# Projection slots of the next batch moved by one attention step, and the experts' input scaling moved by two

## What is computed

```python
xn = layernorm(x)
# s: an attention block with a linear recurrence beside it
h = layernorm(xn) * ln1_g + ln1_b
q, k, v = heads(h @ WQ + bQ), heads(h @ WK + bK), heads(h @ WV + bV)   # 16 heads of 8
attn = softmax(where(0 <= i - j < 128, q @ k.T / sqrt(8), -inf))
states = scan(s = A * s + (h @ Bw)_t)
g = sigmoid(h @ Wg + bg)
x1 = xn + g * (attn @ v @ WO + bO) + (1 - g) * (states @ Cw)
s = x1 + gelu(layernorm(x1) @ W1 + b1) @ W2 + b2
# f: top 2 of 8 experts on the rms-normed bfloat16 input nf
f = xc + sum_e combine_e * (act(nf @ mlp1_e) @ mlp2_e)
out = x + s * silu(f)
```

## Time and profile before

| | us |
|---|---|
| median of three runs | 1056.16 |
| lowest and highest of them | 1053.68, 1056.58 |
| the profiled execution | 1053.38 |
| its span, first to last instruction | 1051.6 |

### The profile page before, as it was taken

How to read it: one execution, slowest core, us unless ns; L and a number is a source line. 1 busy time by engine, 2 the same in 40 slices (tenths; PEclk the granted TensorE clock), 3 DMA queues, 4 the chain that set the end, 5 groups by cost and what they waited for, 6 DMA issues and landing times.

```text
span 1051.6 us, 38097 instructions
## 1 busy us (share of the span) xinstructions
PE 901.4 (86%) x15768; PEld 554.8 (53%) x15768; DVE 726.6 (69%) x1747; ACT 742.0 (71%) x1302; POOL 500.0 (48%) x786
## 2 busy tenths in 40 slices
PE   2486999989889898989999998989989898988896
PEld 1243564645556464555556464555646455554535
DVE  8255687777768677777768677876858687766415
ACT  3224787867868786777878787776868677766755
POOL 6323547272644627364554727363553736433331
PEclk7556999999999999999999999999999899999969
DMA  5743513434160333425151333425142242510000
GB/s 103 141 99 63 112 31 107 53 106 65 48 124 19 111 53 102 66 77 96 47 115 29 109 55 103 65 78 94 48 103 31 93 66 67 96 37 7 26 2 11
DMA packets 85598, 75.15 MB, mean 71 GB/s; under 512 B 9458, under 2 KB 79155, under 8 KB 85427
## 3 DMA queue, kind: packets, MB, share of 16 engines
q1 hardware_dynamic: 83346, 71.93, 31.6%
q10 hardware_dynamic: 2080, 0.79, 0.3%
HBM read 36.26 MB, written 30.15 MB: 63 GB/s over the span
## 4 chain that ended last, share of the span: by engine, by line
PE 50%; DVE 21%; issue 14%; ACT 10%; DMA 2%; POOL 1%; SPq 1%; DVEq 0%; POOLq 0%; ACTq 0%
PE ps L567 7%; PE ps L507 6%; PE ps L705 5%; PE ps L765 5%; PE ps L726 5%; PE ps L496 4%; ACT pt L862 3%; DVE mx L1111 3%; DVE gc L1162 3%; DVE lin L1155 2%; PE ps L584 2%; PE ps L699 2%; PE ps L579 2%; PE ps L597 2%; PE ps L522 2%
## 5 line engine op out<-in xcount | busy, mean ns | idle before, releaser
L1111 DVE TENSOR_REDUCE mx<-ps 128x2 f32<-128x320 f32 (+1 forms) x512 | 226.4, 467 | 140.9 <-PE ps L522 136.2
L862 ACT ACTIVATE pt<-ps 128x1024 f32<-128x1024 f32 (+1 forms) x256 | 234.6, 916 | 124.8 <-PE ps L496 124.0
L1284 POOL TENSOR_SCALAR_AFFINE_SELECT pt<-pt 128x512 f32<-128x512 f32 x256 | 164.2, 643 | 228.0 <-ACT pt L862 227.6
L507 PE MATMUL ps<-kd,qz 48*32 48x160 bf16 (+1 forms) x4096 | 154.9, 240 | 68.1 <-DVE mx L1111 38.7
L496 PE MATMUL ps<-qz,kd 51*32 51x256 bf16 (+1 forms) x4096 | 176.3, 273 | 4.8 <-ACT pt L862 2.8
L507 PEld LDWEIGHTS ps<-kd,qz 48*32 48x32 bf16 x4096 | 77.9, 92 | 187.1 <-ACT pt L862 95.5
L567 PE MATMUL ps<-pt,va 128*32 128x256 f32 (+1 forms) x2048 | 157.9, 389 | 5.1 <-issue 4.5
L705 PEld LDWEIGHTS ps<-m,act_t 128*128 128x128 f32 x1024 | 126.8, 191 | 51.4 <-DVE act_t L1183 36.4
L705 PE MATMUL ps<-m,act_t 128*128 128x128 f32 x1024 | 143.2, 283 | 8.5 <-DVE act_t L1183 8.0
L1287 POOL TENSOR_SCALAR_AFFINE_SELECT pt<-pt 128x512 f32<-128x512 f32 x192 | 129.3, 674 | 0.0
L920 ACT ACTIVATE lin<-ps,mbias 128x512 f32<-128x512 f32 x128 | 87.6, 684 | 47.5 <-DVE act_t L1183 29.6
(11 more groups left out here) (172 smaller groups left out, 1630.4 us busy)
## 6 DMA issues: line engine op xcount, KB each, us to landing
qz<-qk_parts SPq DMA_DIRECT2D x32, 384.0 KB, 7.4
kd<-qk_parts SPq DMA_DIRECT2D x32, 384.0 KB, 9.2
qk_parts<-qp SPq DMA_DIRECT2D x16, 384.0 KB, 2.6
qk_parts<-kp SPq DMA_DIRECT2D x16, 384.0 KB, 2.4
xl<-L_attn_x SPq DMA_DIRECT2D x16, 256.0 KB, 3.5
qk_parts<-qp SPq DMA_DIRECT2D x16, 256.0 KB, 3.0
qk_parts<-kp SPq DMA_DIRECT2D x16, 256.0 KB, 2.7
xnr<-xn SPq DMA_DIRECT2D x16, 256.0 KB, 3.2
```

Of the source, the lines that this page charges most:

```text
L507: nc.tensor.matmul(ps[QG * c:QG * (c + 1), 4 + par, w * pr:w * (pr + 1)], qz[q][rows, 2 * g + pr, P * i + QG * c:P * i + QG * (c + 1)], kd ...
L862: nc.scalar.activation(to, src, ACT.Exp, scale=SCALE).then_inc(exp_ok.sem, 1)
L1111: nc.vector.tensor_reduce(mx[:, i, HG * g + pr:HG * (g + 1):2], src, AX.X, ALU.max).then_inc(mx_ok.sem, 1)
L1284: sel1 = nc.gpsimd.affine_select(out=pt[:, s, :, 0:P], in_=pt[:, s, :, 0:P], compare_op=ALU.is_ge, fill=0.0, base=0, pattern=[[0, HG], [1, ...
```

## The change

Two lines of constants. The transpose of h0, q, k, u, v, g and the experts' combine weights are each due one step sooner; `AT_STATES`, the cast, the squares and the root keep their steps; the scaling moves from steps 10 and 11 to 12 and 13. What is placed relative to these moves with them: `qk_rest` from half steps 10 and 14 to 8 and 12, `recur` from 19 to 17, `split_rest` from steps 6 and 8 to 5 and 7. `MIX` is not changed. No instruction is added or removed.

```diff
--- before.py
+++ after.py
@@ -59,8 +59,8 @@
 NEG = -1e30
 TIE = -1e-37
 CONSTS = 4
-AT_STATES, AT_H0, AT_Q, AT_K, AT_U, AT_V, AT_G, AT_C = 0, 2, 4, 6, 8, 10, 12, 14
-AT_CAST, AT_SQ, AT_RS, AT_NF = 4, 6, 8, 10
+AT_STATES, AT_H0, AT_Q, AT_K, AT_U, AT_V, AT_G, AT_C = 0, 1, 3, 5, 7, 9, 11, 13
+AT_CAST, AT_SQ, AT_RS, AT_NF = 4, 6, 8, 12
 AT_H2 = 4
 MIX = (6, 7, 12, 15)
```

## The result

| | before | after |
|---|---|---|
| median, us | 1054.92 (4 runs, 1051.86 to 1056.58) | 1123.52 (4 runs, 1122.43 to 1124.9) |
| profiled execution's span, us | 1051.6 | 1121.9 |
| mean granted clock of the span | 0.932 | 0.921 |

The ratio is 1.065 (95% interval 1.063 to 1.068): slower by 68.6 us. The forecast was 1101.4, and 1118 for the rival in which the clock falls oftener.

The account below looks back on a forecast made before the run. It took a ring of waits among score matmuls, exponentials and maxima as the bound, with TensorE binding only in its long pieces; links summed to 3.43 us per body, 48.0 over 14, added to 1053.38: 1101.4 us, range 1066 to 1124.

Parts of the forecast that it names:

- the clock rival: Rival: every body gets a further fall of TensorE's clock at 1.2 us, 17 us more, 1118 us; chance 0.12.
- start to q: From a body's start to projection q: the transpose waits for s1, and q comes 0.81 us sooner.
- q to k: From projection q to k: a full values piece replaces the short one, 0.13 us longer.
- k to u: From projection k to u: kr, cp and cr delay step 7's second half, +0.71 and 0.65 us on top.
- u to v: From projection u to v: step 9 waits for the long exponential of step 8, 0.07 us longer.
- v to g: From projection v to g: v no longer hides step 10's exponential and the copy of ot, 0.62 us longer.
- g to end: From g to the last values matmuls: one more step, 2.06 us longer, 0.54 of it from the later scaling.
- faster: Rival: the transpose runs in TensorE's idle time, q 1.50 us sooner; -0.3 us per body, 1049 us; chance 0.05.
- cr alone waits: Case between k and u: only cr waits for GpSimd's subtraction, 0.4 us on top.
- both wait: Case between k and u: cp and cr wait for GpSimd and cr meets the next select, 0.93 us on top.
- Much of it is hidden: Rival: cp and cr slip in and the added last step costs 1.2 us; about 1.0 per body, 1067 us; chance 0.06.
- The sum over 14 bodies: Bodies 0 to 13, with attention and projections, each lose 3.43 us, 48.0 us in all; other bodies lose nothing.

Follow-up runs that it names:

- e1: The changed kernel with the experts' scaling back at steps 10 and 11; 1100.7 us, ratio 1.046.
- e6: The changed kernel with GpSimd's split of q one step later, at step 6 in place of 5; 1076.2 us, ratio 1.024.
- e10: The changed kernel with extra unread matmuls only near the start of each body (4 and 3), none at steps 7 and 9; 1101.9 us, ratio 1.045.
- e5: The kernel before with only the transpose of h0 (and hT) one step sooner; 1073.0 us, ratio 1.019.
- e3: The changed kernel with extra unread matmuls in TensorE's idle time, near the start and at steps 7 and 9; 1095.6 us, ratio 1.041.
- e7: The kernel before with extra unread matmuls in TensorE's idle time, at steps 2, 6 and 8; 1047.8 us, ratio 1.000.
- e2: The changed kernel with cp and cr half a step later, at half step 13 in place of 12; 1077.0 us, ratio 1.022.

## Why the prediction held, and where it was off

**The sign and the mechanism of the links were right; the point was not.** 1123.5 lies outside the forecast's own bounds of 1084 to 1110 and only 0.5 us inside the range, which reached to 1124 for the sake of the clock rival. That the range held is partly luck. The signs named in advance came: q 0.7 us sooner in a clean body, k to u 5.75, g to the last values 6.79, exponential 14 right behind cT, and the second half of step 7 released by a maximum behind kr, cp and cr. Set against the clean links of the table, a body's terms, forecast and measured:

```
              start to q   q to k   k to u         u to v   v to g   g to end     sum
forecast        -0.81      +0.13    +0.71 +0.65    +0.07    +0.62    +2.06       +3.43
measured        -0.74      +0.14    +1.57          +0.10    +0.60    +2.0        +3.67
```

Measured is after minus the undisturbed body of before, the parts of the changed kernel taken from its own links where no fall touches them (k to u, v to g, g to next) and from e1 and e6 where one does. The sum makes 61.8 us of 58.1, and e10's clean body is 61.8.

**Start to q.** Right in size: the transpose waits for s, step 2 moves up against it, and q gains 0.8 us and not a whole step. The rival "faster" needed q 1.5 sooner. e5 shows that this edit without q's is a loss.

**k to u.** The mechanism was right, the size short by 0.2. The forecast took 0.65, between "cr alone waits" and "both wait" (0.93). Both waited in 14 of cp's 16 executions, as the subtraction starts 0.08 us ahead of cp, and cp ended 0.04 us behind it each time. The trace of before could have told: there another cast of 32 columns, L1020, meets this subtraction (645.62 to 646.78), ends 0.04 us behind it, and takes 0.9 us in 13 of its 16 executions.

```profile
645.91 0.91 DVE L1020 CAST cp<-cr 128x32 bf16<-128x32 f32 x1
```

In the changed kernel that cast meets no such instruction and takes 0.17. The Trainium skill's statement ("GPSIMD Engine Reference", section 1, Specifications) that the two engines share SBUF interfaces fits the trace and e6: 1.11 us with GpSimd's two-input instruction beside it, 0.17 without.

**v to g and g to the end.** Right to 0.1 us. Of the 2.0 us, 0.43 are the scaling's (e1; forecast 0.54), the rest is the added step, bound by exponentials.

**"Much of it is hidden" and "faster"** did not happen: no link but the first shrank.

**The clock is the step that was mis-sized.** The point of 1101.4 left it where it was; the rival had it at 1118 with a chance of 0.12. The mean body is 4.81 us longer (64.95 - 60.14), 3.67 by the links; the remaining 1.1 us, 16 us in the run, is a net figure. After, falls cost 64.95 - 61.8 = 3.2 us in a body; before, falls and stalls cost 60.14 - 58.1 = 2.0, and 1.0 of that are stalls, as its clean bodies average 59.1. So falls cost about 1.0 us in a body before and 3.2 after, and nearly half of that increase is offset by stalls that do not show in the changed kernel. That the net is close to the rival's 1.2 is luck: it priced one further fall, and no such stalls. The forecast should have counted the change's idle gaps, 1.1 us ahead of the transpose and 2.3 in step 7, as likely to bring a fall in each body. I had seen one body fall and its twin not, and gave the rival a small chance for it. The forecast also had the places right only in part: the shorter fall comes behind the gap in step 7, as it said, but the longer one comes at the start, and none in steps 11 to 15. What the Trainium skill says of short idling between groups of matmuls ("TensorE: Matmul & The Clock Gate", section "A second HAM failure mode: psum-queue depth-cycling") did bear here: e3 agrees, with no fall once the gaps are filled. It does not settle a single body, as 4 of e1's 14 have the same gaps and no time at half clock.

**The sum over 14 bodies** was right in the main: 67.3 of the 70.2 us between the two traces lie in them, and what stands ahead of and behind them grew by 1.8 and 1.1 us, which the forecast had at nothing.

## What to carry to other kernels

When steps of a hand-ordered pipeline are moved, sum the links between the moved pieces, and ask of each which wait ends last. Shifting a whole chain one step sooner buys only what its first link gives, and it adds a step behind its last. Two moves that look apart can meet on one engine: here a relative slot (kr) ran into an absolute one (cp, cr), beside a GpSimd instruction that moved along, and that one collision was over 40% of the loss by links. Look for a like pair in the trace of before: here L1020 had shown what cp would cost. Judge such a change by clean bodies first, then look at the granted clock, as idle time that costs little by itself can cost again as much through it.

## What the hardware showed that I had not expected

- Work added can save time. Some 16 matmuls of 512 columns in each body, in TensorE's idle time, took 28 us off 1123.5 (e3); the clock stayed at full in all 14 bodies. In the kernel before the same fill gave nothing that can be measured (e7).
- The clock can multiply other gains and losses. Removing 6 us by the links gave 23 (e1), 23 gave 46 (e2), 18 gave 47 (e6). The falls that went in e1 were not near the edit. Which body gets a fall with the same gaps stays open.
- A cast of 32 columns took 0.17 or 1.11 us with nothing moved but the GpSimd instruction beside it (e6), and in the changed kernel it ended 0.04 us behind that instruction in 14 executions.
- TensorE stalls of 0.8 to 2 us without a releaser come in many bodies, at places that differ between kernels (u to v 3.72 or 4.61). Their cause was not tested. The medians of the kernel before differ by 5 us between sessions (1049.9 to 1054.9).
